# Mixture of experts: rows stored by slot and gathered back, in place of accumulating DMAs

## The chip, the cores and the metric

The kernel runs on one core of a Trainium2 chip. A core has five engines that work side by side and meet at semaphores: TensorE (PE) multiplies matrices, VectorE (DVE) and ScalarE (ACT) do elementwise work, GpSimd (POOL) does elementwise work and issues DMAs whose addresses come from a table in SBUF, and SyncE (SP) issues plain DMAs. The metric is the device time of one execution, in microseconds (us); the median of several runs counts.

## The reference

The network is a chain of six residual layers over 1024 tokens of 256 floats: mixture of experts, attention, mixture of experts, sparse feed-forward, a state-space layer, sparse feed-forward. The change touches the mixture of experts, which runs twice. The reference computes it like this, `x` being the normalised tokens:

```python
E, TOPK, H, I = (8, 2, 256, 512)
logits = SOFTCAP * jnp.tanh(x @ w_gate / SOFTCAP)
probs = jax.nn.softmax(logits, axis=-1)
_, idx = jax.lax.top_k(probs, TOPK)
mask = jax.nn.one_hot(idx, E, dtype=probs.dtype).sum(-2)
weights = probs * mask
for e in range(E):
    h = jax.nn.silu(x @ w1[e]) * (x @ w3[e])
    out = out + h @ w2[e] * weights[:, e:e + 1]
# and outside: x = x + 0.5 * layer(layernorm(x))
```

Each token so gets the sum of two experts' outputs, and only these two are needed.

## The kernel before

`moe_layer` runs only the experts that were picked. The 1024 tokens times 2 picks are sorted by expert into 23 items (`ITEMS`) of 128 slots each; each expert's last item is filled up with spare slots. A slot belongs to one (token, pick) pair. The layer has these stages:

1. VectorE makes the normalised tokens `xn` (L315). POOL stores them in DRAM as `rows` (L266). SP stores the residual in DRAM as `sums` (L253) and then loads the weights of all eight experts, 24 DMAs of 512 KB (L256, L258).
2. The router (L318 to L389) works out for every (token, pick) its slot (`slot`, L365), and from it three tables by slot: `token`, the token number or a spare row, `slot_w`, its weight, and `expert_of`, the expert of each item.
3. The item loop. POOL gathers an item's 128 token rows by an indirect DMA (`gather`, L272, four items ahead at most). TensorE turns them (L506), multiplies by the gate and up weights (L511), turns the product (L533) and multiplies by the down weights (L541). ScalarE and VectorE stand between these steps (L437, L443, L397, L449). VectorE weighs the 128 output rows into `y` (`weigh`, L406; two buffers), and POOL adds them into `sums` in DRAM by an accumulating indirect DMA (`add_rows`, L282). Two such adds may touch the same token, so each waits until the one before has landed (`summed`, L281).
4. When all 23 adds have landed, SP loads `sums` back into the residual (L261), and VectorE takes the statistics for the next layer's normalisation (`token_stats`, L75), eight tiles of 128 tokens.

TensorE starts its first multiplication only when all 24 weight loads have landed (`pe.wait_ge(q[loaded], 16 * EXPERTS)`). Each layer is a block of its own: no engine enters the next layer's block before all have left this one. On each engine instructions run in the order in which they are written. `routing_tables` prepares constants, and stores zeros in the spare rows of `rows` and `sums` (L2343).

Of the kernel before, what the change touches and what calls it, by code (L numbers as in the profile page):

```python
# [9 lines left out]
F32 = mybir.dt.float32  # L10
F32R = mybir.dt.float32r
BF16 = mybir.dt.bfloat16
U32 = mybir.dt.uint32
I32 = mybir.dt.int32
ALU = mybir.AluOpType
# [3 lines left out]
P = 128  # L19
D = 256  # L20
S = 1024
TT = S // P
# [143 lines left out]
CHOICES = 2  # L166
# [4 lines left out]
AHEAD = 4  # L171


def moe_layer(nc, xres, stats, ident, route, w_gate, w1, w3, w2, rows, sums, pool_dma, tag):

# [4 lines left out]
    with ExitStack() as ctx:  # L182
# [26 lines left out]
        place = sp.sb("place", [P, TT, EXPERTS])  # L209
        slot1 = sp.sb("slot1", [P, PICKS])  # L210
        slot = sp.sb("slot", [P, PICKS], I32)
        slot_item = sp.sb("slot_item", [P, PICKS], I32)
        slot_row = sp.sb("slot_row", [P, PICKS], I32)
        in_row = sp.sb("in_row", [P, PICKS, P], F32R)
# [18 lines left out]
        xT_ps = sp.ps("xT", [P, BANK])  # L233
        hT_ps = sp.ps("hT", [P, KI, P])
        out_ps = [sp.ps(f"out{b}", [P, BANK]) for b in range(2)]
        turn_banks = [gate_ps[0], gate_ps[1], up_ps[0], up_ps[1]]
        logit_ps, rank_ps, total_ps, slot_ps = out_ps[0], out_ps[1], xT_ps, hT_ps

        names = ("wg_loaded", "gate_loaded", "up_loaded", "down_loaded", "sums_stored",
                 "eps_done", "mv_done", "std_done", "rstd_done", "xn_done", "turned", "xnT_done", "logits_done",  # L240
                 "capped_done", "exp_done", "router", "both_done", "totals_done", "ranks_done",
                 "row_done", "send_done", "slots_done", "expert_done", "token_done", "slot_w_done",
                 "x_turned", "xT_done", "gate_done", "up_done", "silu_done", "h_done", "h_turned",
                 "hT_done", "out_done", "y_done", "reloaded")
        q = {n: sp.sem(n) for n in names}
        gathered, rows_stored, summed = pool_dma["gathered"], pool_dma["rows_stored"], pool_dma["summed"]
        ctx.callback(sp.clear_sems)
        block = ctx.enter_context(nc.Block())

        @block.sync  # L250
        def _(sync):
            sync.dma_start(wg[:], w_gate.rearrange("(k p) e -> p k e", p=P)).then_inc(q["wg_loaded"], 16)
            sync.dma_start(sums[0:S, :].rearrange("(t p) d -> p t d", p=P), xres).then_inc(q["sums_stored"], 16)  # L253
            for e in range(EXPERTS):
                for name, src, loaded in (("gate_up", w1, "gate_loaded"), ("up", w3, "up_loaded")):
                    sync.dma_start(w_in[name][:, e * KD:(e + 1) * KD, :], src[e].rearrange("(k p) n -> p k n", p=P)  # L256
                                   ).then_inc(q[loaded], 16)
                sync.dma_start(w_dn[:, e * KI:(e + 1) * KI, :], w2[e].rearrange("(k p) n -> p k n", p=P)  # L258
                               ).then_inc(q["down_loaded"], 16)
            sync.wait_ge(summed, 16 * ITEMS)  # L260
            sync.dma_start(xres, sums[0:S, :].rearrange("(t p) d -> p t d", p=P)).then_inc(q["reloaded"], 16)  # L261

        @block.gpsimd
        def _(pool):
            pool.wait_ge(q["xn_done"], TT)
            nc.gpsimd.dma_start(rows[0:S, :].rearrange("(t p) d -> p t d", p=P), xn[:]).then_inc(rows_stored, 16)  # L266

            def gather(i):
                b = i % AHEAD
                if i >= AHEAD:  # L270
                    pool.wait_ge(q["x_turned"], i - AHEAD + 1)
                nc.gpsimd.indirect_dma_start(out=xg[b][:], out_offset=None, in_=rows[:, :],  # L272
                                             in_offset=bass.IndirectOffsetOnAxis(ap=token[:, i:i + 1], axis=0)
                                             ).then_inc(gathered[b], 16)

            def add_rows(i):
                pool.wait_ge(q["y_done"], i + 1)
                if i == 0:
                    pool.wait_ge(q["sums_stored"], 16)
                else:  # L280
                    pool.wait_ge(summed, 16 * i)  # L281
                nc.gpsimd.indirect_dma_start(out=sums[:, :],  # L282
                                             out_offset=bass.IndirectOffsetOnAxis(ap=token[:, i:i + 1], axis=0),
                                             in_=y[i % 2][:], in_offset=None, compute_op=ALU.add
                                             ).then_inc(summed, 16)

            pool.wait_ge(rows_stored, 16)
            pool.wait_ge(q["token_done"], 1)
            for i in range(AHEAD):
                gather(i)  # L290
            for i in range(ITEMS):
                add_rows(i)
                if i + AHEAD < ITEMS:
                    gather(i + AHEAD)

        @block.vector
        def _(dve):
# [64 lines left out]
                                                ALU.mult, ALU.add))  # L362
            then(nc.vector.tensor_tensor(share[:], pick[:], place[:].unsqueeze(1).broadcast_to(cells), ALU.mult))
            then(nc.vector.tensor_reduce(slot1[:], share[:].rearrange("p k t e -> p (k t) e"), AX_X, ALU.add))
            then(nc.vector.tensor_scalar(slot[:], slot1[:], -1.0, None, ALU.add))  # L365
            nc.vector.tensor_scalar(slot_row[:], slot[:], P - 1, None, ALU.bitwise_and).then_inc(q["router"], 1)
            nc.vector.tensor_scalar(slot_item[:], slot[:], 7, None, ALU.logical_shift_right).then_inc(q["router"], 1)
# [31 lines left out]
            def weigh(i):  # L399
                b = i % 2  # L400
                dve.wait_ge(q["out_done"], i + 1)
                if i == 0:
                    dve.wait_ge(q["slot_w_done"], 1)
                if i >= 2:
                    dve.wait_ge(summed, 16 * (i - 1))
                nc.vector.tensor_scalar(y[b][:], out_ps[b][:, 0:D], slot_w[:, i:i + 1], None, ALU.mult).then_inc(q["y_done"], 1)  # L406

            for i in range(ITEMS):
# [1 line left out]
                if i:  # L410
                    weigh(i - 1)
            weigh(ITEMS - 1)
            dve.wait_ge(q["reloaded"], 16)
            token_stats(nc, stats, xres, range(TT))

        @block.scalar
        def _(act):
# [1896 lines left out]
def routing_tables(nc, keep, xres, ident, stats, x, ident_in, triangle, places):  # L2314
# [2 lines left out]
    route = dict(places=keep.sb("places", [P, P]), token1=keep.sb("token1", [P, PICKS]), spare1=keep.sb("spare1", [P, 1]),  # L2317
                 fills=keep.sb("fills", [P, EXPERTS]), ones=keep.sb("ones", [P, EXPERTS]),
                 ones_bf=keep.sb("ones_bf16", [P, P], BF16), upper=keep.sb("upper", [P, P], BF16))
    route["dram"] = [[nc.dram_tensor(f"moe{n}_{what}", (ROWS, D), F32).ap() for what in ("rows", "sums")] for n in range(2)]  # L2320
    with ExitStack() as ctx:
        sp = Space(nc, ctx, "main")
        eights = sp.sb("eights", [P, EXPERTS])
# [10 lines left out]
        @block.sync  # L2334
        def _(sync):
            sync.dma_start(xres[:], x.rearrange("b (t p) d -> p (b t) d", p=P)).then_inc(loaded, 16)
            sync.dma_start(ident[:], ident_in).then_inc(loaded, 16)
            sync.dma_start(eights[:], places.partition_broadcast(P)).then_inc(loaded, 16)
            sync.dma_start(upper_f[:], triangle).then_inc(upper_in, 16)
            sync.wait_ge(cleared, 1)  # L2340
            for n in range(2):
                for scratch in route["dram"][n]:
                    sync.dma_start(scratch[S:ROWS, :], zeros[:]).then_inc(spare_rows, 16)  # L2343
            sync.wait_ge(loaded, 48)
            sync.wait_ge(spare_rows, 64)

        @block.gpsimd
        def _(pool):
# [21 lines left out]
def macaron_kernel(nc, x, out, ident_in, triangle, mask, places, cos_t, sin_t, moe_gate, moe_w1, moe_w3, moe_w2,  # L2370
                   w_qkv, w_o, ffn_gate, ffn_up, ffn_down, in_w, conv_w, conv_b, dt_bias, a_log, d_skip, norm_w, out_w):
    with ExitStack() as ctx:
        sp = Space(nc, ctx, "main")
        xres = sp.sb("residual", [P, TT, D])
        ident = sp.sb("ident", [P, P])
        stats = sp.sb("token_stats", [P, TT, 6])
        stored = sp.sem("stored")
        pool_dma = [dict(gathered=[sp.sem(f"moe{n}_gathered{b}") for b in range(AHEAD)],
                         rows_stored=sp.sem(f"moe{n}_rows_stored"), summed=sp.sem(f"moe{n}_summed")) for n in range(2)]
        with ExitStack() as routing:  # L2380
            route = routing_tables(nc, Space(nc, routing, "route"), xres, ident, stats, x, ident_in, triangle, places)
            moe = (moe_gate, moe_w1, moe_w3, moe_w2)
            moe_layer(nc, xres[:], stats[:], ident[:], route, *moe, *route["dram"][0], pool_dma[0], "moe0")
            attention_layer(nc, xres[:], stats[:], ident[:], cos_t, sin_t, w_qkv, w_o, "attn")
            moe_layer(nc, xres[:], stats[:], ident[:], route, *moe, *route["dram"][1], pool_dma[1], "moe1")
        sparse_ffn_layer(nc, xres[:], stats[:], ident[:], ffn_gate, ffn_up, ffn_down, "ffn0")
        mamba_layer(nc, xres[:], stats[:], ident[:], triangle, mask, in_w, conv_w, conv_b, dt_bias, a_log, d_skip, norm_w,
                    out_w, "ssm")
        sparse_ffn_layer(nc, xres[:], stats[:], ident[:], ffn_gate, ffn_up, ffn_down, "ffn1", is_last=True)

        with nc.Block() as block:
            @block.sync
            def _(sync):
                sync.dma_start(out.rearrange("b (t p) d -> p (b t) d", p=P), xres[:]).then_inc(stored, 16)
                sync.wait_ge(stored, 16)
# [42 lines left out]
```

## Time and profile before

| what | us |
|---|---|
| median of 3 runs (lowest, highest) | 1891.13 (1887.7, 1897.0) |
| the profiled execution's own time | 1888.53 |
| its span (first to last instruction) | 1886.6 |
| PE busy | 1592.8 (84%) |
| DVE busy | 1151.1 (61%) |
| ACT busy | 862.5 (46%) |
| POOL busy | 440.5 (23%) |

All starts in the rows below are microseconds from the span's start, and durations are those of this one execution. The first mixture-of-experts layer lies at 10.5 to 208, the second at 721.5 to 920. "Idle before" in square brackets is how long the engine had stood idle and whose end released it. PEclk is the granted clock of TensorE: 1.00 is 2.4 GHz, 0.50 is 1.2 GHz.

### The profile page before, as it was taken

Reading aid. Unit: us, or ns where it says so; the run is one execution under the profiler, and the core shown is the slowest. Engines: PE = TensorE matmul, PEld = TensorE weight load, DVE = VectorE, ACT = ScalarE, POOL = GpSimd, SP = SyncE. Lnnn points to the kernel's source line nnn. Section 1 sums busy time; section 2 is a strip of 40 time slices with the busy share of each in tenths; the row PEclk is TensorE's granted clock in tenths of the full one; section 3 lists DMA queues with packets and bytes.
Section 4 is the critical chain, followed back from the end, with each engine's and each line's share of the span. In section 5 each row is a group of like instructions: output and inputs, shape, how many; then the busy total and the mean of one; then the engine's idle time right before and its main releaser. Section 6 shows DMA issues by size and latency. Waiting matters only on the chain. (4 is left out here: it accounts for less than half of the span.)

```text
span 1886.6 us, 25249 instructions
## 1 busy us (share of the span) xinstructions
PE 1592.8 (84%) x8136; PEld 1136.7 (60%) x8136; DVE 1151.1 (61%) x2072; ACT 862.5 (46%) x1270; POOL 440.5 (23%) x358
## 2 busy tenths in 40 slices
PE   3899389999999994799487786899999989988686
PEld 3466244454444444466376675787878878877575
DVE  3112578887878844121388574676776676675586
ACT  1122226665556571122232665666665666564232
POOL 1243320000000001244200111444444345343100
PEclk9999769999999996899798897999999999999798
DMA  8322110000000007322300100100100000010200
GB/s 306 76 47 44 43 23 8 5 12 12 11 12 11 0 1 241 102 47 43 98 1 0 40 17 13 29 18 23 29 18 23 26 13 28 12 29 12 67 1 23
DMA packets 70247, 73.78 MB, mean 39 GB/s; under 512 B 8384, under 2 KB 56896, under 8 KB 70144
## 3 DMA queue, kind: packets, MB, share of 16 engines
q1 hardware_dynamic: 60768, 58.35, 10.2%
q0 software_dynamic: 9376, 14.16, 4.3%
q8 instruction: 51, 0.84, 0.2%
q14 instruction: 52, 0.43, 0.1%
HBM read 56.50 MB, written 11.80 MB: 36 GB/s over the span
## 5 line engine op out<-in xcount | busy, mean ns | idle before, releaser
L779 DVE TENSOR_REDUCE attn_max_halves<-attn_scores 128x1 f32<-128x512 f32 x470 | 302.5, 686 | 69.8 <-PE attn_scores L1003 62.2
L908 ACT ACTIVATE attn_probs<-attn_scoresT 128x1024 f32<-128x1024 f32 x256 | 253.3, 1025 | 171.2 <-PE attn_scoresT L1016 170.8
L1003 PE MATMUL attn_scores<-attn_k_picks,attn_qT_pass 128*128 128x512 f32 x470 | 197.7, 452 | 5.7 <-DVE attn_max_halves L779 3.5
L1003 PEld LDWEIGHTS attn_scores<-attn_k_picks,attn_qT_pass 128*128 128x128 f32 x470 | 81.6, 188 | 152.4 <-DVE attn_max_halves L779 146.7
L1016 PE MATMUL attn_scoresT<-attn_qT_pass,attn_k_picks 128*128 128x512 f32 x512 | 168.7, 404 | 0.8 <-DVE attn_max_halves L779 0.8
L397 DVE TENSOR_TENSOR moe_h<-moe_silu,moe_up 128x512 f32<-128x512 f32 x46 | 31.6, 688 | 212.0 <-PE moe_up L511 212.0
L1442 DVE SCALAR_TENSOR_TENSOR ssm_scan_x<-ssm_scan_proj,ssm_w_conv,ssm_scan_x 128x1023 f32<-128x1023 f32 (+2 forms) x96 | 122.9, 1280 | 60.2 <-ACT ssm_scan_x L1437 57.1
L1030 PE MATMUL attn_o<-attn_probs,attn_v_group 128*32 128x512 f32 x1024 | 136.4, 605 | 0.6 <-ACT attn_probs L908 0.6
L443 ACT ACTIVATE moe_silu<-moe_gate 128x512 f32<-128x512 f32 x46 | 27.5, 598 | 223.1 <-PE moe_gate L511 223.1
L62 PE MATMUL ssm_scan_proj<-ssm_xnT_hi,ssm_w_in_hi 128*128 128x512 f32 x256 | 115.3, 450 | 5.6 <-POOL ssm_scan_mask L1920 5.4
L282 POOL DMA_INDIRECT moe_sums<-moe_y,moe_token x46 | 73.1, 1588 | 188.4 <-DVE moe_y L406 182.1
L2270 PE MATMUL ssm_scan_out<-ssm_scan_w_out,ssm_scan_v 128*128 128x256 f32 x464 | 114.1, 394 | 2.7 <-issue 2.7
L511 PE MATMUL moe_gate<-moe_w_gate_up,moe_xT 128*128 x184 | 90.3, 614 | 24.5 <-DMA moe_w_down<-in_moe_w 12.3
L2137 ACT ACTIVATE ssm_scan_decay<-ssm_scan_cum,ssm_neg_cum 128x128 f32<-128x128 f32 x256 | 73.3, 369 | 76.5 <-PE ssm_scan_cum L2207 76.5
L1016 PEld LDWEIGHTS attn_scoresT<-attn_qT_pass,attn_k_picks 128*128 128x128 f32 x512 | 93.9, 188 | 22.4 <-ACT attn_probs L908 4.4
L64 PE MATMUL ssm_scan_proj<-ssm_xnT_hi,ssm_w_in_lo 128*128 128x512 f32 x256 | 105.6, 412 | 0.0
L63 PE MATMUL ssm_scan_proj<-ssm_xnT_lo,ssm_w_in_hi 128*128 128x512 f32 x256 | 105.5, 412 | 0.0
L2270 PEld LDWEIGHTS ssm_scan_out<-ssm_scan_w_out,ssm_scan_v 128*128 128x128 f32 x464 | 91.5, 199 | 16.1 <-issue 2.8
L1924 POOL TENSOR_TENSOR ssm_w_in_lo<-ssm_w_in,ssm_w_in_hi 128x512 fp32r<-128x512 f32 x31 | 42.3, 1365 | 235.1 <-ACT ssm_w_in_hi L2101 235.1
L541 PE MATMUL moe_out<-moe_w_down,moe_hT 128*128 x368 | 87.1, 380 | 1.5 <-ACT moe_hT L449 1.5
L2026 DVE SCALAR_TENSOR_TENSOR ssm_scan_x<-ssm_scan_x,ssm_d_skip,ssm_scan_y 128x1024 f32<-128x1024 f32 x32 | 41.0, 1280 | 77.5 <-PE ssm_scan_y L2248 77.5
L541 PEld LDWEIGHTS moe_out<-moe_w_down,moe_hT 128*128 128x128 f32 x368 | 69.8, 190 | 30.2 <-issue 23.1
(338 smaller groups left out, 3414.5 us busy)
## 6 DMA issues: line engine op xcount, KB each, us to landing
moe_w_gate_up<-in_moe_w SPq DMA_DIRECT2D x16, 512.0 KB, 11.3
moe_w_up<-in_moe_w SPq DMA_DIRECT2D x16, 512.0 KB, 11.1
moe_w_down<-in_moe_w SPq DMA_DIRECT2D x16, 512.0 KB, 11.4
ssm_w_in<-in_in_w SPq DMA_DIRECT2D x64, 128.0 KB, 2.2
attn_k_picks<-attn_kT SPq DMA_DIRECT2D x32, 128.0 KB, 2.4
ssm_scan_w_out<-in_out_w SPq DMA_DIRECT2D x8, 512.0 KB, 4.1
moe_sums<-main_residual SPq DMA_DIRECT2D x2, 1024.0 KB, 5.7
moe_rows<-moe_xn POOLq DMA_DIRECT2D x2, 1024.0 KB, 9.9
```

The source lines that it names most:

```text
L62: nc.tensor.matmul(out, lhs_hi, rhs_hi, start=start, stop=False)
L63: nc.tensor.matmul(out, lhs_hi, rhs_lo, start=False, stop=False)
L64: return nc.tensor.matmul(out, lhs_lo, rhs_hi, start=False, stop=stop)
L511: last = nc.tensor.matmul(bank[:].unsqueeze(1), xT[i % 2][:, k, :], w_in[name][:, bass.ds(e * KD + k, 1), :], start=(k == 0), stop=(k == K ...
L541: last = nc.tensor.matmul(out_ps[i % 2][:, 0:D].unsqueeze(1), hT[i % 2][:, k, :], w_dn[:, bass.ds(e * KI + k, 1), :], start=(k == 0), stop ...
L779: return nc.vector.tensor_reduce(rmax2[:, t, j, c:c + 1], chunk_bank(g, n), AX_X, ALU.max).then_inc(reduced, 1)
L908: nc.scalar.activation(probs[s % 2][:, 2 * pair:2 * pair + 2, :], st_ps[pair][:], ACT.Exp, scale=SCALE).then_inc(exp_done, 1)
L1003: nc.tensor.matmul(chunk_bank(g, n), qm[b][:, t * P:(t + 1) * P], kz[b][:, j, c * BANK:(c + 1) * BANK], start=True, stop=True).then_inc(sc ...
L1016: last = nc.tensor.matmul(st_ps[pair][:, j % 2, :], kz[b][:, j, kt * P:(kt + 1) * P], qe[b][:, half * BANK:(half + 1) * BANK], start=True, ...
L1030: last = nc.tensor.matmul(o_ps[j * STACK:(j + 1) * STACK, :], vg[b][:, kt, :], probs[s % 2][:, j, :], start=(kt == 0), stop=(kt == KT_TILE ...
L1442: return nc.vector.scalar_tensor_tensor(out[:, shift:], ps[:, :S - shift], w(k), out[:, shift:], ALU.mult, ALU.add)
L2270: last = nc.tensor.matmul(out[:, m, :], v[:, v_row(b * NORM_HEADS + jn), cols], w_out[:, jn, :], start=(jn == 0), stop=(jn == NORM_HEADS - 1))
```

## The change

The residual no longer goes to DRAM. `sums` is replaced by a DRAM tensor `slots` with one row for each of the 23 x 128 slots. SP stores each weighted item `y` there by a plain DMA (23 of 128 KB), with a semaphore for each of the two buffers. POOL first issues all gathers of token rows; when all items are stored, it gathers, for each of the eight token tiles, the two slots of each token (`take_back`, 16 indirect DMAs of 128 rows) into SBUF that the layer no longer needs (`xn` and `xnT`). VectorE then adds the two rows to the residual, tile by tile, and takes each tile's statistics. The router writes `slot1 - 1` once more, as an unsigned integer, for these gathers.

```diff
-            sync.dma_start(sums[0:S, :].rearrange("(t p) d -> p t d", p=P), xres).then_inc(q["sums_stored"], 16)
...
-            sync.wait_ge(summed, 16 * ITEMS)
-            sync.dma_start(xres, sums[0:S, :].rearrange("(t p) d -> p t d", p=P)).then_inc(q["reloaded"], 16)
+            for i in range(ITEMS):
+                sync.wait_ge(q["y_done"], i + 1)
+                sync.dma_start(slots[i * P:(i + 1) * P, :], y[i % 2][:]).then_inc(y_stored[i % 2], 16)
+            for b in range(2):
+                sync.wait_ge(y_stored[b], 16 * ((ITEMS + 1 - b) // 2))
...
-            def add_rows(i):
-                pool.wait_ge(q["y_done"], i + 1)
-                if i == 0:
-                    pool.wait_ge(q["sums_stored"], 16)
-                else:
-                    pool.wait_ge(summed, 16 * i)
-                nc.gpsimd.indirect_dma_start(out=sums[:, :],
-                                             out_offset=bass.IndirectOffsetOnAxis(ap=token[:, i:i + 1], axis=0),
-                                             in_=y[i % 2][:], in_offset=None, compute_op=ALU.add
-                                             ).then_inc(summed, 16)
+            def take_back(t, k):
+
+                at = k * TT + t
+                nc.gpsimd.indirect_dma_start(out=picked[k][:, t, :], out_offset=None, in_=slots[:, :],
+                                             in_offset=bass.IndirectOffsetOnAxis(ap=slot_u[:, at:at + 1], axis=0)
+                                             ).then_inc(combined[t], 16)
...
-            for i in range(ITEMS):
-                add_rows(i)
-                if i + AHEAD < ITEMS:
-                    gather(i + AHEAD)
+            for i in range(AHEAD, ITEMS):
+                gather(i)
+            for b in range(2):
+                pool.wait_ge(y_stored[b], 16 * ((ITEMS + 1 - b) // 2))
+            for t in range(TT):
+                for k in range(CHOICES):
+                    take_back(t, k)
...
+            nc.vector.tensor_scalar(slot_u[:], slot1[:], -1.0, None, ALU.add)
             then(nc.vector.tensor_scalar(slot[:], slot1[:], -1.0, None, ALU.add))
...
                 if i >= 2:
-                    dve.wait_ge(summed, 16 * (i - 1))
+                    dve.wait_ge(y_stored[b], 16 * (i // 2))
...
-            dve.wait_ge(q["reloaded"], 16)
-            token_stats(nc, stats, xres, range(TT))
+            for t in range(TT):
+                dve.wait_ge(combined[t], 32)
+                for k in range(CHOICES):
+                    then(nc.vector.tensor_tensor(xres[:, t, :], picked[k][:, t, :], xres[:, t, :], ALU.add))
+                token_stats(nc, stats, xres, (t,))
...
-                for scratch in route["dram"][n]:
-                    sync.dma_start(scratch[S:ROWS, :], zeros[:]).then_inc(spare_rows, 16)
+                sync.dma_start(route["dram"][n][0][S:ROWS, :], zeros[:]).then_inc(spare_rows, 16)
```

SP at the start of the first layer, before: the store of the residual stands ahead of the weights.

```order
L252 DMA moe0_w_gate<-in_moe_gate 128x2x8
L253 DMA moe0_sums<-main_residual 128x8x256
L256 DMA moe0_w_gate_up<-in_moe_w1 128x2x512
L256 DMA moe0_w_up<-in_moe_w3 128x2x512
L258 DMA moe0_w_down<-in_moe_w2 128x4x256
```

The same place after.

```order
L255 DMA moe0_w_gate<-in_moe_gate 128x2x8
L258 DMA moe0_w_gate_up<-in_moe_w1 128x2x512
L258 DMA moe0_w_up<-in_moe_w3 128x2x512
L260 DMA moe0_w_down<-in_moe_w2 128x4x256
```

One DMA of 1024 KB is gone from the head of the queue; the 24 weight loads follow in the same order.

POOL at the end of the first layer, before: the last gather of token rows (`x_rows`) and the accumulating DMAs.

```order
L272 DMA moe0_x_rows2<-moe0_rows,moe0_token 128x256 [waits moe0_x_turned]
L282 DMA moe0_sums<-moe0_y1,moe0_token 1152x256 [waits main_moe0_summed,moe0_y_done]
L282 DMA moe0_sums<-moe0_y0,moe0_token 1152x256 [waits main_moe0_summed,moe0_y_done]
L182 UNCONDITIONAL_BRANCH
L49 UNCONDITIONAL_BRANCH [waits barrier_Pool_Activation_PE_DVE_SP_gather]
```

The same place after, the first two of the 16 gathers back (into `xn` and `xnT`).

```order
L277 DMA moe0_x_rows2<-moe0_rows,moe0_token 128x256 [waits moe0_x_turned]
L284 DMA moe0_xn<-moe0_slots,moe0_slot_u 128x256 [waits moe0_y_stored1,moe0_y_stored0]
L284 DMA moe0_xnT<-moe0_slots,moe0_slot_u 128x256
L182 UNCONDITIONAL_BRANCH
L49 UNCONDITIONAL_BRANCH [waits barrier_Pool_Activation_PE_DVE_SP_gather]
```

Of the 16 gathers the first pair stands here; the pair is issued eight times, and only its first instruction waits. All of them stand behind the last item's store.

VectorE at the end of the first layer, before.

```order
L406 TENSOR_SCALAR moe0_y0<-moe0_out0,moe0_slot_w 128x256 [waits main_moe0_summed,moe0_out_done]
L75 BN_STATS main_token_stats<-main_residual 128x6 [waits moe0_reloaded]
L75 BN_STATS main_token_stats<-main_residual 128x6 x7
L182 UNCONDITIONAL_BRANCH
L758 UNCONDITIONAL_BRANCH [waits barrier_Pool_Activation_PE_DVE_SP_release]
```

The same place after, with the last of the eight tiles.

```order
L411 TENSOR_SCALAR moe0_y0<-moe0_out0,moe0_slot_w 128x256 [waits moe0_y_stored0,moe0_out_done]
...
L421 TENSOR_TENSOR main_residual<-moe0_xn,main_residual 128x256 [waits main_moe0_combined7]
L421 TENSOR_TENSOR main_residual<-moe0_xnT,main_residual 128x256 [waits moe0_router]
L75 BN_STATS main_token_stats<-main_residual 128x6 [waits moe0_router]
L182 UNCONDITIONAL_BRANCH
L766 UNCONDITIONAL_BRANCH [waits barrier_Pool_Activation_PE_DVE_SP_release]
```

The eight statistics waited for one load; now each tile has its own wait, two additions and its statistics.

## Rows read from the trace of the kernel before

**Rows 1.** The page's part 1: busy time and share of each engine.
```profile
PE 1592.8 (84%) x8136; PEld 1136.7 (60%) x8136; DVE 1151.1 (61%) x2072; ACT 862.5 (46%) x1270; POOL 440.5 (23%) x358
```

**Rows 2.** Item loop: stretch, PE, PEld, DVE, ACT, POOL busy, PEclk, DMA share, GB/s.
```profile
100.00:150.00 50.00, 50.00 (x189) 31.47 (x188) 10.54 (x18) 10.98 (x25) 21.34 (x17) 1.00 0.30 48
```

**Rows 3.** Timeline of one item of the loop: start, duration, engine, line.
```profile
73.64 1.88 PE L511 MATMUL moe_gate<-moe_w_gate_up,moe_xT 128*128 x4
73.85 0.48 DVE L406 TENSOR_SCALAR moe_y<-moe_out,moe_slot_w 128x256 f32<-128x256 f32 x1 [0.99 <-PE moe_out L541]
...
74.61 1.60 POOL L282 DMA_INDIRECT moe_sums<-moe_y,moe_token  x1 [2.89 <-DVE moe_y L406]
...
76.51 0.98 POOL L272 DMA_INDIRECT moe_x_rows<-moe_rows,moe_token  x1 [0.30 <-PE moe_xT L506]
...
79.46 1.02 PE L511 MATMUL moe_gate<-moe_w_gate_up,moe_xT 128*128 x2
```

**Rows 4.** Timeline, start of both layers: residual store, first gate multiplication.
```profile
10.96 0.46 SPq L253 DMA_DIRECT2D moe_sums<-main_residual  x1
...
56.45 1.21 PE L511 MATMUL moe_gate<-moe_w_gate_up,moe_xT 128*128 x1 [12.23 <-issue]
...
767.48 3.78 PE L511 MATMUL moe_gate<-moe_w_gate_up,moe_xT 128*128 x4 [12.30 <-DMA moe_w_down<-in_moe_w]
```

**Rows 5.** Busy time by stretch, while the weights load; the last column is GB/s.
```profile
12.00:16.00 4.00, 2.62 (x13) 2.62 (x14) 3.03 (x10) 1.69 (x5) 0.21 (x1) 1.00 0.97 262
20.00:55.00 35.00, 8.95 (x52) 8.16 (x51) 11.85 (x61) 2.14 (x4) 3.90 (x4) 1.00 1.03 363
723.00:727.00 4.00, 2.61 (x12) 2.61 (x13) 3.03 (x10) 1.70 (x5) 0.21 (x1) 0.50 1.01 283
```

**Rows 6.** Timeline, end of the first layer.
```profile
193.17 0.48 DVE L406 TENSOR_SCALAR moe_y<-moe_out,moe_slot_w 128x256 f32<-128x256 f32 x1 [2.71 <-PE moe_out L541]
...
195.33 1.55 POOL L282 DMA_INDIRECT moe_sums<-moe_y,moe_token  x1 [3.04 <-DMA moe_sums<-moe_y,moe_token]
199.01 0.37 SPq L261 DMA_DIRECT2D main_residual<-moe_sums  x1
204.59 2.71 DVE L75 BATCH_NORM_STATS2 main_token_stats<-main_residual 128x6 f32<-128x256 f32 x8 [10.93 <-DMA main_residual<-moe_sums]
```

**Rows 7.** Timeline, end of the second layer.
```profile
916.91 2.71 DVE L75 BATCH_NORM_STATS2 main_token_stats<-main_residual 128x6 f32<-128x256 f32 x8 [11.06 <-DMA main_residual<-moe_sums]
```

**Rows 8.** Timeline, first layer: the token table, and three of the first four gathers.
```profile
36.48 0.18 DVE L387 SCALAR_TENSOR_TENSOR moe_token<-moe_hT,moe_empty 128x24 uint32<-128x24 f32 x1
...
37.55 1.05 POOL L272 DMA_INDIRECT moe_x_rows<-moe_rows,moe_token  x1 [20.63 <-DVE moe_token L387]
...
38.91 0.95 POOL L272 DMA_INDIRECT moe_x_rows<-moe_rows,moe_token  x1 [0.30 <-issue]
...
41.42 0.95 POOL L272 DMA_INDIRECT moe_x_rows<-moe_rows,moe_token  x1 [0.30 <-issue]
```

**Rows 9.** DMA issues: size of each, median us from issue to landing.
```profile
ssm_w_in<-in_in_w SPq DMA_DIRECT2D x64, 128.0 KB, 2.2
...
out<-main_residual SPq DMA_DIRECT2D x1, 1024.0 KB, 4.4
...
moe_x_rows<-moe_rows,moe_token POOLq DMA_INDIRECT x46, 2.8
...
moe_rows<-main_zeros SPq DMA_DIRECT2D x2, 128.0 KB, 4.0
```

**Rows 10.** Instructions on VectorE by shape: busy total, mean ns of one.
```profile
L1226 DVE TENSOR_TENSOR ffn_xT_lo<-ffn_xT,ffn_xT_hi 128x256 fp32r<-128x256 f32 x16 | 6.7, 418 | 0.1
```

**Rows 11.** One line's instructions: ns min/median/max, first and last start.
```profile
L118 DVE TENSOR_SCALAR attn_xn<-main_residual,attn_ln_mean_var,attn_ln_rstd x8: 395/407/5366, 214.1 to 221.5; 128x256 f32<-128x256 f32 x8
```

**Rows 12.** Busy time by stretch where TensorE restarts after the layer; PEclk third from the end.
```profile
222.00:224.00 2.00, 2.00 (x10) 2.00 (x10) 1.81 (x3) 1.47 (x3) 0.00 (x0) 0.51 0.00 0
224.00:226.00 2.00, 1.85 (x11) 1.52 (x9) 1.45 (x4) 0.44 (x3) 0.00 (x0) 1.00 0.00 0
```

More of the change, by code:

```diff
@@ L171, with moe_layer @@
 AHEAD = 4
-def moe_layer(nc, xres, stats, ident, route, w_gate, w1, w3, w2, rows, sums, pool_dma, tag):
+def moe_layer(nc, xres, stats, ident, route, w_gate, w1, w3, w2, rows, slots, pool_dma, tag):
     with ExitStack() as ctx:
@@ L211, in moe_layer @@
         slot = sp.sb("slot", [P, PICKS], I32)
+        slot_u = sp.sb("slot_u", [P, PICKS], U32)
         slot_item = sp.sb("slot_item", [P, PICKS], I32)
@@ L235, in moe_layer @@
         out_ps = [sp.ps(f"out{b}", [P, BANK]) for b in range(2)]
+        picked = [xn, xnT[:].rearrange("p k (a d) -> p (k a) d", d=D)]
         turn_banks = [gate_ps[0], gate_ps[1], up_ps[0], up_ps[1]]
         logit_ps, rank_ps, total_ps, slot_ps = out_ps[0], out_ps[1], xT_ps, hT_ps
-        names = ("wg_loaded", "gate_loaded", "up_loaded", "down_loaded", "sums_stored",
+        names = ("wg_loaded", "gate_loaded", "up_loaded", "down_loaded",
                  "eps_done", "mv_done", "std_done", "rstd_done", "xn_done", "turned", "xnT_done", "logits_done",
@@ L243, in moe_layer @@
                  "x_turned", "xT_done", "gate_done", "up_done", "silu_done", "h_done", "h_turned",
-                 "hT_done", "out_done", "y_done", "reloaded")
+                 "hT_done", "out_done", "y_done")
         q = {n: sp.sem(n) for n in names}
-        gathered, rows_stored, summed = pool_dma["gathered"], pool_dma["rows_stored"], pool_dma["summed"]
+        y_stored = [sp.sem(f"y_stored{b}") for b in range(2)]
+        gathered, rows_stored, combined = pool_dma["gathered"], pool_dma["rows_stored"], pool_dma["combined"]
         ctx.callback(sp.clear_sems)
@@ L2319, in routing_tables @@
                  ones_bf=keep.sb("ones_bf16", [P, P], BF16), upper=keep.sb("upper", [P, P], BF16))
-    route["dram"] = [[nc.dram_tensor(f"moe{n}_{what}", (ROWS, D), F32).ap() for what in ("rows", "sums")] for n in range(2)]
+    route["dram"] = [[nc.dram_tensor(f"moe{n}_{what}", (size, D), F32).ap() for what, size in (("rows", ROWS), ("slots", ITEMS * P))]
+                     for n in range(2)]
     with ExitStack() as ctx:
@@ L2341, in _ @@
             for n in range(2):
-                for scratch in route["dram"][n]:
-                    sync.dma_start(scratch[S:ROWS, :], zeros[:]).then_inc(spare_rows, 16)
+                sync.dma_start(route["dram"][n][0][S:ROWS, :], zeros[:]).then_inc(spare_rows, 16)
             sync.wait_ge(loaded, 48)
-            sync.wait_ge(spare_rows, 64)
+            sync.wait_ge(spare_rows, 32)
         @block.gpsimd
@@ L2378, in macaron_kernel @@
         pool_dma = [dict(gathered=[sp.sem(f"moe{n}_gathered{b}") for b in range(AHEAD)],
-                         rows_stored=sp.sem(f"moe{n}_rows_stored"), summed=sp.sem(f"moe{n}_summed")) for n in range(2)]
+                         rows_stored=sp.sem(f"moe{n}_rows_stored"), combined=[sp.sem(f"moe{n}_combined{t}") for t in range(TT)]) for n in range(2)]
         with ExitStack() as routing:
```

## The prediction, made before the changed kernel ran

> **What bounds the kernel now.** I read the page's busy times first: TensorE is busy 84% of the span [rows 1]. That average says little here, because each layer is closed off from the next; so I looked at the three stages of a mixture-of-experts layer.
>
> The item loop comes first. The stretches show TensorE busy 50.00 of 50 us, with POOL at 21.34 and DMA at 0.30 [rows 2]. From one item's gate multiplication (73.64) to the next (79.46) go 5.82 us, and in them POOL's add and gather end at 77.49, so it then stands idle until the next `y` [rows 3]. TensorE alone sets the pace; the 23 adds are hidden, except the last.
>
> The start is next. TensorE's first multiplication starts at 56.45 after 12.23 us of idleness, in the second layer at 767.48, released by the last weight load [rows 4]. Until then the DMA engines are full, at 363 GB/s [rows 5]. What the DMA engines carry ahead of the last weight moves this start.
>
> Last the end. The last `y` is ready at 193.65 (193.17 + 0.48). Its add is issued at 195.33, because the add before it must have landed; it lands before 199.01, where SP issues the load; the statistics start at 204.59 and end at 207.30 [rows 6]. So 13.65 us pass with TensorE idle; in the second layer VectorE stands idle for 11.06 us before its statistics, the first 10.93 [rows 6, 7]. No engine does other work there: every microsecond of this chain is on the path.
>
> **The change, part by part.**
>
> *Start: the store of the residual goes.* Its 1024 KB head the queue (issued at 10.96, [rows 4]). From 12 to 16 the DMA engines move 262 GB/s x 4 us = 1.05 MB, just this store's size; in the second layer 1.13 MB in the 4 us from 723 [rows 5]. So the store holds the queue for about 4 us, and the weights follow it. The least that it can be worth is its bytes at the later rate, 1.05 MB / 363 GB/s = 2.9 us; the most is those 4.0 us plus some of its issue, 4.3. I take 3.6 for each layer, nearer to the measured stretch, with a little off since weight reads may already run under its last writes. Two layers: -7.2 us. The start stays bound by the weights: the first four gathers are issued by 42.4 [rows 8], long before.
>
> *The additional `slot_u` and the two missing stores of zeros: 0.* `slot_u` delays the token table by 0.1 to 0.2 us, at 36.66 [rows 8]; the weights, for which TensorE waits until 56.45, hide it, 3.6 us of gain included. If they didn't, it would cost 0.2 us a layer. The zeros are queued behind the loads for which the first statistics wait; gone, they are worth at least 0 and at most the 0.5 us of an issue.
>
> *Loop: adds out of POOL, stores into SP: 0.* POOL has idle time already. `weigh` of item i now waits for the store of item i-2, 11.6 us earlier (2 x 5.82), which takes 2 to 4 us. Behind a late one would queue VectorE's next product, and TensorE behind that; the cover is about 7 us. SP has nothing else to issue by then. I exclude a gain because TensorE has no idle time to give back [rows 2].
>
> *End: add, wait and reload go; store, 16 gathers and additions come.* The new chain in the first layer, with before's times for what comes ahead:
>
> - The store of the last `y` (128 KB, plain, SP). The trace has no such store alone. From below: the 1024 KB store of the output lands in 4.4, less the 0.92 MB more that it moves, 2.5 us at 363 GB/s, is 1.9. From above: the 128 KB stores of zeros at the start, queued behind others, take 4.0. A 128 KB load takes 2.2 [rows 9]. I take 2.3: landed at 195.95.
> - POOL sees it. From a `y` ready at 74.33 to its add at 74.61 pass 0.28 us [rows 3]; from the token table (36.66) to the first gather 0.89 [rows 8]. I take 0.6: first gather at 196.55.
> - Sixteen gathers. They are the same operation as those of token rows (128 rows of 1 KB). Queued one behind the other these start 1.255 us apart (38.91 to 41.42, two steps), 0.95 busy and 0.30 between; both steps are POOL's own, since nothing is waited for [rows 8]. The last starts 15 x 1.255 = 18.8 us after the first, at 215.4. From below, the 0.30 could vanish: 0.95 each. From above, each could take as long as an accumulating one, 1.60 [rows 3] and 0.30: 1.9.
> - The last lands 2.8 after its issue [rows 9], at 218.2.
> - The last tile's two additions and statistics. The nearest addition, 128x256, takes 0.418 [rows 10], with a semaphore between I take 0.45; the statistics 2.71 / 8 = 0.34, say 0.4 alone. Together 1.3: 219.5. The other seven tiles' work (1.3 every 2.5 us) lies under the gathers.
>
> 219.5 against 207.30 is +12.2 us for a layer, +24.4 for both. Everything after it (the barrier, the next layer) follows with the same distances.
>
> The clock: TensorE restarts after the layer at 1.2 GHz (0.51 of 222 to 224) and is at 2.4 GHz from 224 [rows 12]. It had fallen in the idle time already, so 12 us more of idleness add nothing I can price; one such ramp, four microseconds at half the clock, is the size of error that I allow.
>
> **Sum.** 24.4 - 7.2 = +17.2 us on the profiled execution's 1888.5 gives 1905.7. Its span is 1886.6, and the 1.9 around it stays. That execution lies 2.6 us under the median of the three runs, 1891.1; from the median the sum would be 1908.3. I predict 1907, between.
>
> **A rule of the skill against the row.** The row shows a gather every 1.255 us [rows 8]. The Trainium skill, page "DMA: Bandwidth & Descriptors", section "Anatomy of one DMA — SWDGE (gpsimd) path", says that descriptor generation is small and that the cost of a DMA is a fixed 2 us, mostly the wait for the write's receipt, plus bytes over 436 GB/s. By that rule the 16 gathers would overlap and take only what their bytes take, an estimate of 16 x 0.3 us. The trace doesn't agree for gathers by index; the case stands among the rivals.
>
> **The rivals.**
>
> *Data-bound gathers (faster).* If 16 queued gathers were paced by their data and not by POOL, at 128 KB (0.131 MB) / 363 GB/s = 0.36 us each, the last would be issued 5.4 us after the first in place of 18.8: each layer 13.4 us shorter, and the sum 17.2 - 26.8 = -9.6, 1879 on the profiled base. It speaks for it that the DMA engines are idle then; against it that POOL is busy 0.95 us for each gather even where nothing holds it, 0.95 and 1.05 at the start, 0.98 in the loop [rows 3, 8]. The page named above would give this case.
>
> *Gathers at their busy time (no change that can be told).* With 0.95 each and no gap, 15 x 0.305 x 2 = 9.2 less: +8.0, about 1897 to 1899. For it: the gap is called "issue", nothing known. Against: it stands in both steps, and 0.30 also in the loop. The change only pays below 0.68 us a gather, where the 15 steps save the 8.6 us (12.2 - 3.6) by which each layer else grows.
>
> *Gathers and additions hinder each other (slower still).* In the new tail, and nowhere before, gathers run beside VectorE additions with both inputs in SBUF. One `attn_xn` took 5.366 us against a median of 0.407 [rows 11], so some instructions of VectorE and POOL do shut each other out. If each gather lost one addition's time (0.42), 15 x 0.42 x 2 = 12.6 more: 1920. The Trainium skill, page "SBUF — State Buffer", section "Who interferes with whom", says that such a tensor_tensor contends with GpSimd's reads, while descriptor generation needs the write side; by that nothing is lost.
>
> *Only a few gathers may be in flight.* Four in a row is all that the trace shows. Were each to wait for the one before to land, 2.8 in place of 1.255: 15 x 1.55 x 2 = 46 more, 1953.
>
> *The weights don't come earlier.* If the start stayed where it is, 7.2 more: 1914. It is part of the forecast's range.
>
> **How the numbers follow.** The forecast has 0.75; its own terms leave 1898 to 1915 (start 2.9 to 4.3, store 1.9 to 4.0, pick-up 0.3 to 0.9, each twice; the gathers' step a tenth either way is 3.8; the base 2.6). Hindered gathers 0.07, few in flight 0.03; gathers without the gap 0.10; data-bound 0.05. The range reaches down to the case without the gap and up to the hindered one: 1896 to 1919. A measurement of this kernel can tell a change from about 0.5%, 9.5 us, on: below 1881.7 is faster, over 1900.6 slower. Faster 0.05; within 0.11 (the gapless case and the forecast's lower edge); slower 0.84.
>
> **What would show it.** The first gate multiplication would start 3.6 us earlier (about 52.9), items still every 5.8 us; from the last `y` to the end of the last statistics 25.9 us in place of 13.65; 16 gathers 1.25 us apart, each waiting for nothing; SP's stores of `y` landing in about 2.3; VectorE idle before each tile's first addition, released by a gather. The forecast is wrong if the gathers' step is under 0.8 or over 1.6, or if the item loop slows down.

## The result, and the profile after

The changed kernel takes 1913.68 us (median; 1912.06 to 1915.51), the kernel before beside it 1889.7. The ratio is 1.0099, with a 95% interval of 1.0072 to 1.0127; the two medians alone give 1.0127, the edge of it. Timed again later, six runs beside 17 of before, it is 1.0114 (1.0086 to 1.0143). So the change costs about 1%, some 20 us. Of 17 executions of the kernel before that were timed with the first four variants below, four were slow ones of 2712 to 5370 us; no ratio counts them. The profiled execution took 1913.1 us, with a span of 1911.3.

First the start of both layers after the change, from the timeline; it answers to [rows 4].

```profile
11.04 0.46 SPq L258 DMA_DIRECT2D moe_w_gate_up<-in_moe_w  x1
...
53.55 3.77 PE L519 MATMUL moe_gate<-moe_w_gate_up,moe_xT 128*128 x4 [12.04 <-issue]
...
779.22 1.21 PE L519 MATMUL moe_gate<-moe_w_gate_up,moe_xT 128*128 x1 [13.21 <-DMA moe_w_down<-in_moe_w]
```

The weights' first DMA is now at the head of the queue, and the first gate multiplication starts at 53.55, where it was 56.45. The second layer as a whole lies later now, so it is measured from its own start below.

The item loop by stretch: stretch, PE, PEld, DVE, ACT and POOL busy, PEclk, DMA share, GB/s.

```profile
100.00:150.00 50.00, 50.00 (x192) 31.32 (x191) 9.86 (x17) 11.72 (x26) 7.64 (x9) 1.00 0.14 45
```

TensorE is as full as in [rows 2]. POOL has 7.64 us of work in place of 21.34, and DMA 0.14 in place of 0.30, but the loop is no shorter.

The end of the first layer, timeline of POOL and VectorE; it answers to [rows 6].

```profile
191.07 0.48 DVE L411 TENSOR_SCALAR moe_y<-moe_out,moe_slot_w 128x256 f32<-128x256 f32 x1 [2.71 <-PE moe_out L549]
193.53 0.95 POOL L284 DMA_INDIRECT moe_xn<-moe_slots,moe_slot_u  x1 [36.78 <-DMA moe_slots<-moe_y]
194.78 0.95 POOL L284 DMA_INDIRECT moe_xnT<-moe_slots,moe_slot_u  x1 [0.30 <-issue]
196.04 0.95 POOL L284 DMA_INDIRECT moe_xn<-moe_slots,moe_slot_u  x1 [0.30 <-issue]
197.30 0.95 POOL L284 DMA_INDIRECT moe_xnT<-moe_slots,moe_slot_u  x1 [0.30 <-issue]
197.56 0.42 DVE L421 TENSOR_TENSOR main_residual<-moe_xn,main_residual 128x256 f32<-128x256 f32 x1 [6.00 <-DMA moe_xnT<-moe_slots,moe_slot_u]
198.01 0.42 DVE L421 TENSOR_TENSOR main_residual<-moe_xnT,main_residual 128x256 f32<-128x256 f32 x1
198.47 0.43 DVE L75 BATCH_NORM_STATS2 main_token_stats<-main_residual 128x6 f32<-128x256 f32 x1
198.55 0.96 POOL L284 DMA_INDIRECT moe_xn<-moe_slots,moe_slot_u  x1 [0.30 <-issue]
...
212.44 0.96 POOL L284 DMA_INDIRECT moe_xnT<-moe_slots,moe_slot_u  x1 [0.30 <-issue]
...
215.26 0.42 DVE L421 TENSOR_TENSOR main_residual<-moe_xn,main_residual 128x256 f32<-128x256 f32 x1 [1.27 <-DMA moe_xnT<-moe_slots,moe_slot_u]
215.72 0.42 DVE L421 TENSOR_TENSOR main_residual<-moe_xnT,main_residual 128x256 f32<-128x256 f32 x1
216.18 0.43 DVE L75 BATCH_NORM_STATS2 main_token_stats<-main_residual 128x6 f32<-128x256 f32 x1
218.05 0.21 POOL L728 MEMSET attn_k_stack<- 128x128 f32 x1 [4.66 <-POOLq L48]
```

The 16 gathers stand in one row, 1.26 us apart, and wait for nothing; VectorE finishes a tile and idles until the next pair lands. From the last `y` (191.55) to the end of the statistics (216.61) pass 25.06 us, where it was 13.65. TensorE idles through all of it.

DMA issues of the changed kernel: size, median us from issue to landing.

```profile
moe_slots<-moe_y SPq DMA_DIRECT2D x46, 128.0 KB, 1.7
```

Now the whole span in stages, each from its first VectorE instruction to that of the next. The four untouched layers are taken together.

| stage, us | before | after | difference |
|---|---|---|---|
| first mixture-of-experts layer | 197.53 | 207.44 | +9.91 |
| second | 198.84 | 206.87 | +8.03 |
| both | 396.37 | 414.31 | +17.94 |
| attention, feed-forward twice, state space | 1479.66 | 1486.31 | +6.65 |

Within the two layers: block start to first gate multiplication -3.0 and -2.1; item loop +0.8 and -1.4; last `y` to end of statistics +11.4 and +11.2; from there to the next block +0.7 and +0.3. So the layers that were changed give 17.9 us. The 6.7 us more (6.8 in the expectations below, from starts read to 0.1 us) lie in layers whose code is the same, and had to be explained.

### The profile page after: what moved, and what is told of

It reads as the page before. It is cut to its first block and busy times, and to the rows that moved or that the text cites. A ratio compares the mean times of both kernels' runs of the same rounds, so it can differ in the third digit from the quotient of the medians.

```text
span 1911.3 us, 25269 instructions
## 1 busy us (share of the span) xinstructions
PE 1591.0 (83%) x8136; PEld 1133.5 (59%) x8136; DVE 1164.6 (61%) x2106; ACT 862.7 (45%) x1270; POOL 397.7 (21%) x344
## 5 line engine op out<-in xcount | busy, mean ns | idle before, releaser
L277 POOL DMA_INDIRECT moe_x_rows<-moe_rows,moe_token x46 | 44.0, 956 | 235.6 <-PE moe_xT L514 198.1
## 6 DMA issues: line engine op xcount, KB each, us to landing
moe_w_up<-in_moe_w SPq DMA_DIRECT2D x16, 512.0 KB, 11.2
moe_w_down<-in_moe_w SPq DMA_DIRECT2D x16, 512.0 KB, 11.2
```

## The experiments

Three variants of the changed kernel ask what paces the gathers. In each, the times meant are those from the last `y` to the end of the statistics.

**One pick only.** 8 gathers a layer.

```diff
-                for k in range(CHOICES):
-                    take_back(t, k)
+                take_back(t, 0)
...
-                dve.wait_ge(combined[t], 32)
-                for k in range(CHOICES):
+                dve.wait_ge(combined[t], 16)
+                for k in range(1):
```

> The changed kernel with only the first pick gathered back and added: 8 gathers a layer in place of 16; the second pick's rows are left out of the result. Theory (POOL paces the gathers, 1.26 us each): from the last y to the end of the last statistics 25.1 - 8 x 1.26 - 0.45 = 14.5 us in each layer, the whole some 21 us shorter than the changed kernel's 1913, 1892. Rival (the tail is mostly store, wake-up and landing, with the gathers overlapping): the tail shrinks by 4 us or less in each layer.

Measured: 14.54 and 14.44 us, and 1893.1 as a whole (one run). 25.0 - 14.5 = 10.5 us for 8 gathers and one addition of 0.45: 1.26 each. The theory's numbers held: each gather less makes the tail one step shorter.

**Half the bytes.** The table of slots then counts half rows.

```diff
-                nc.gpsimd.indirect_dma_start(out=picked[k][:, t, :], out_offset=None, in_=slots[:, :],
+                nc.gpsimd.indirect_dma_start(out=picked[k][:, t, 0:P], out_offset=None, in_=slots.rearrange("r (h d) -> (r h) d", h=2),
...
-            nc.vector.tensor_scalar(slot_u[:], slot1[:], -1.0, None, ALU.add)
+            nc.vector.tensor_scalar(slot_u[:], slot1[:], 2.0, -2.0, ALU.mult, ALU.add)
```

> The changed kernel, with each of the 16 gathers moving only the first 512 bytes of each row (128 rows as before; the other half of each row is left out of the result). Theory (POOL's work per instruction or per row sets the pace): the step stays 1.26 us and the tail 25 us. Rival (data-bound gathers): the step falls towards 0.65 us, the tail to some 16 us.

The gathers of this variant on POOL: ns min/median/max.

```profile
L284 POOL DMA_INDIRECT moe_xn<-moe_slots,moe_slot_u x16: 953/955/957, 192.3 to 935.7; - x16
L284 POOL DMA_INDIRECT moe_xnT<-moe_slots,moe_slot_u x16: 952/955/1186, 193.5 to 937.0; - x16
```

Measured: 0.955 busy with the same 0.30 between (one gather in each layer took 1.2, cause not known), and 24.97 and 25.03 us from the last `y` to the end. The whole is 1912.3 (one run). Half the data saves nothing. Data-bound gathers are refuted.

**Half the rows.**

```diff
-                nc.gpsimd.indirect_dma_start(out=picked[k][:, t, :], out_offset=None, in_=slots[:, :],
-                                             in_offset=bass.IndirectOffsetOnAxis(ap=slot_u[:, at:at + 1], axis=0)
+                nc.gpsimd.indirect_dma_start(out=picked[k][0:64, t, :], out_offset=None, in_=slots[:, :],
+                                             in_offset=bass.IndirectOffsetOnAxis(ap=slot_u[0:64, at:at + 1], axis=0)
```

> The changed kernel with gathers of 64 rows of 1 KB in place of 128 (the other 64 tokens of each tile are left out of the result). If POOL pays by the row, 0.95 busy becomes about 0.5 and the step 0.8 us, the tail 25.1 - 15 x 0.47 = 18 us. If it pays by the instruction, the step stays 1.26. Data-bound gathers would give the first result too, so it counts only beside the run with half the bytes.

The same rows of this variant:

```profile
L284 POOL DMA_INDIRECT moe_xn<-moe_slots,moe_slot_u x16: 904/908/912, 193.9 to 935.9; - x16
L284 POOL DMA_INDIRECT moe_xnT<-moe_slots,moe_slot_u x16: 910/914/918, 195.1 to 937.1; - x16
```

Measured: 0.91 busy for 64 rows against 0.957 for 128, and the tail 24.08 and 24.03; the whole is 1918.6 (one run; its untouched layers took 1493.1, which the last part of this section is about). By these two points 64 rows cost 0.05 us and the instruction itself about 0.86, with 0.30 before the next. POOL pays by the instruction. Each gather here takes one index per partition, 128 rows, so 2048 rows are 16 instructions; a gather of more rows is in no run.

Two experiments take the start apart.

**Late store, in the kernel before.** Only this line moves behind the weights' loop.

```diff
-            sync.dma_start(sums[0:S, :].rearrange("(t p) d -> p t d", p=P), xres).then_inc(q["sums_stored"], 16)
             for e in range(EXPERTS):
...
+            sync.dma_start(sums[0:S, :].rearrange("(t p) d -> p t d", p=P), xres).then_inc(q["sums_stored"], 16)
             sync.wait_ge(summed, 16 * ITEMS)
```

> The kernel before, with the residual's 1024 KB store issued after the 24 weight loads in place of ahead of them; nothing else changes. Theory (the start pays the store's bytes at the queue's rate): the first gate multiplication starts 2.9 us earlier in each layer, the store lands before the first add at 65, and the whole is 5.8 us (0.3%) shorter than before. Rival (the earlier start came from elsewhere in the change, the queue refills the gap): no more than 1 us. Rival 2 (the first add must now wait for the store): the item loop starts late and the gain is lost.

The first gate multiplication of both layers, timeline:

```profile
53.64 2.92 PE L511 MATMUL moe_gate<-moe_w_gate_up,moe_xT 128*128 x3 [9.43 <-issue]
...
762.68 3.78 PE L511 MATMUL moe_gate<-moe_w_gate_up,moe_xT 128*128 x4 [8.79 <-DMA moe_w_down<-in_moe_w]
```

Measured: block start to first gate multiplication 43.10 and 42.35 us, where before has 45.84 and 45.86: 2.7 and 3.5 earlier. The item loop isn't held up by the store (136.92 and 137.38 long, before 137.21 and 138.38). The ratio to before is 0.9981 (0.9960 to 1.0002); 0.9969 was expected and lies inside, but so does no change, just. The stage shows the gain; the whole is too noisy to.

**The store put back, in the changed kernel.**

```diff
+            sync.dma_start(rows_spare[0:S, :].rearrange("(t p) d -> p t d", p=P), xres).then_inc(q["sums_stored"], 16)
             for e in range(EXPERTS):
...
+            sync.wait_ge(q["sums_stored"], 16)
             for b in range(2):
```

> The changed kernel with the residual's 1024 KB store put back ahead of the weights (into a DRAM tensor nobody reads). Theory: the first gate multiplication starts 2.9 us later in the first layer and 2 to 3 later in the second, the whole 5 to 6 us over the changed kernel (about 1919). Rival (the weights' start doesn't depend on the store): same as the changed kernel.

Measured: first multiplication after 46.25 and 45.97 us, where the changed kernel has 42.87 and 43.77: 3.4 and 2.2 later. The tail stays (25.05, 24.98), and the two changed layers take 419.7 us, 5.3 over the changed kernel. The median of four runs is 1917.3, 1.0120 of before (1.0095 to 1.0144). Beside the changed kernel it wasn't timed, and that interval overlaps the changed kernel's: again the stage shows the store, and the whole doesn't. Its untouched layers took 1478.4 us.

That last number was the first sign on the 6.7 us: a variant of the changed kernel whose untouched layers are as short as before's.

**Idle time added to the kernel before**, to move the later layers to where the changed kernel has them.

```diff
-            sync.wait_ge(summed, 16 * ITEMS)
+            sync.wait_ge(q["padded"], 1)
...
+            pool.wait_ge(summed, 16 * ITEMS)
+            cells = {"moe0": 11550, "moe1": 9330}[tag]
+            for at in range(0, cells, 4096):
+                idle = w_in["up" if at < 8192 else "gate_up"][:].rearrange("p a n -> p (a n)")
+                last = nc.gpsimd.memset(idle[:, at % 8192:at % 8192 + min(4096, cells - at)], 0.0)
+            last.then_inc(q["padded"], 1)
```

> The kernel before, with idle time added to the end of both layers: after the last add has landed POOL clears 11550 columns (9.9 us) in the first and 9330 (8.0 us) in the second before SP may reload. That brings the next layers to nearly the same places in time as in the changed kernel. The layers nobody touched (attention, both feed-forward layers, state space) took 6.8 us more in the changed kernel's profile than before. Theory (the granted clock falls at other moments when these layers start later): they take some us more than before here too, 3 to 8, and the whole is 21 to 26 us over before. Rival (the change itself slows them, by its code, its DMAs or where its data lies): they take before's time within 1 us and the whole is 18 us over. Rival 2 (chance from run to run): either, and the runs of one kernel spread by as much.

The second variant has 5800 and 4650 columns in the place of 11550 and 9330.

> As the run with idle time, with half as much (5.0 and 4.0 us). Theory (clock): the untouched layers again differ from before's by several us, not necessarily half as much and of either sign. Rival (the change itself): 0 within 1 us, the whole 9 us over before.

Measured: with 10 us of idleness the two padded layers take 208.2 and 207.4, the untouched ones 1489.6, the whole 1.0102 of before (1.0077 to 1.0127), 19.5 us by the medians. With half of it 203.0, 201.9 and 1489.6, the whole 1.0056 (1.0034 to 1.0078). The whole doesn't decide: 19.5 us lies between the 18 of the rival and the 21 to 26 of the theory, and the interval reaches both, also for the half (10.5 us by the medians, where the rival said 9). The profiles say more. The untouched layers are 10 us over the first profile of before, in a kernel with none of the change's DMAs, and just as much with half the delay. So such a growth needs no part of the change. But "as much for either delay" also speaks against a fixed effect of where the layers start, and for chance. The same two programs, profiled again, test that.

> The kernel before, profiled once more. Its four untouched layers took 1479.6 us in the first profile, and 1484.1 to 1489.6 in the four variants of it. Theory (chance: the moments at which the granted clock falls and rises differ from run to run): some 1485, with 5 either way, not 1479.6 again; the changed layers 197.5 and 198.9 within 1.5. Rival (each program has its own fixed pattern): 1479.6 within 1 us.

> The changed kernel, profiled once more and timed beside the kernel before. Theory (chance): untouched layers some 1485 us with 5 either way, as in the kernel before; over many runs the changed kernel is longer by the changed layers' 17.9 us alone, a ratio of 1.0095. Rival (the change slows the untouched layers): 1486 or more again, and 24 us longer, a ratio of 1.013.

Measured, in the second profiles: the kernel before 198.0 and 197.5, untouched layers 1486.0 (first profile 1479.7). The changed kernel 206.3 and 206.5, untouched layers 1486.5 (first profile 1486.3). The same program thus differs by 6.4 us where nothing was changed, and the second profiles differ by 0.5 there and by 17.3 in the changed layers. The rival of a fixed pattern fell. The 17 executions of before in that series go from 1884.8 to 1898.95, and the ratio of the same program to itself came out as 1.0011 (0.9996 to 1.0025).

The rival that the change slows the untouched layers is not refuted by the whole time: 1.0114 (1.0086 to 1.0143) lies between its 1.013 and the theory's 1.0095, and holds both. The profiles speak against it. The untouched layers took 1479.7 to 1489.7 us in the six of the kernel before and its variants, 1485.6 on average, and 1478.4 to 1493.1 in the six of the changed kernel and its variants, 1486.2 on average. With such a spread an effect of some 5 us can't be excluded, but none is needed.

Where a part of this comes from can be seen in one place, the end of the attention layer, from 506 us after the layer's start on, in both profiles of the kernel before, as busy time by stretch. First profile:

```profile
714.14:721.60 7.46, 3.12 (x24) 2.94 (x24) 4.57 (x11) 0.00 (x0) 0.00 (x0) 1.00 0.00 0
```

Second profile:

```profile
715.00:726.00 11.00, 6.07 (x29) 5.49 (x27) 5.39 (x14) 1.17 (x2) 0.00 (x0) 0.66 0.00 0
```

The columns are as above; PEclk is third from the end. In the first profile TensorE keeps 2.4 GHz to the layer's end; in the second the granted clock is at 1.2 GHz in part of this stretch (0.66 on average). The whole layer takes 516.9 us in place of 513.5. At the stretch's start the second profile is already 1.1 us behind, at the same instruction; 2.3 are lost in the dip. The changed kernel's first profile has the same dip:

```profile
724.12:735.40 11.28, 6.16 (x30) 5.53 (x28) 5.29 (x12) 1.15 (x2) 0.00 (x0) 0.67 0.00 0
```

It is the same short stretch with gaps in TensorE's work; whether the clock falls in it differs between executions of one program. Here too 2.3 us are lost, beside 1.5 before. Of all twelve profiles nine lose 1.5 to 2.3 us in this place: all six of the changed kernel and its variants, and three of the six of before and its variants. It is one place out of several; that the rest of the 6.4 us is of the same kind is likely, but not shown.

**A version that beats both.** The experiments point to keeping the accumulating DMAs, with the late store as above, and a reload in eight DMAs with statistics tile by tile.

```diff
...
-            sync.dma_start(xres, sums[0:S, :].rearrange("(t p) d -> p t d", p=P)).then_inc(q["reloaded"], 16)
+            for t in range(TT):
+                sync.dma_start(xres[:, t, :], sums[t * P:(t + 1) * P, :]).then_inc(reloaded[t], 16)
...
-            dve.wait_ge(q["reloaded"], 16)
-            token_stats(nc, stats, xres, range(TT))
+            for t in range(TT):
+                dve.wait_ge(reloaded[t], 16)
+                token_stats(nc, stats, xres, (t,))
```

> The kernel before with the late store, and the reload cut into eight DMAs of one token tile each, with the statistics of a tile taken as soon as it has landed. Theory: of 2.71 us of statistics only the last 0.4 stay behind the last landing, while eight issues of 0.4 us cost the first landing little: 2 us less for each layer beside the 2.9 of the late store, the whole 9 to 10 us (0.5%) under before. Rival (eight small DMAs land later than one large, by their issue of 8 x 0.42 = 3.4 us): the tail stays within 1 us of before's, and only the late store's gain is left.

The end of its first layer, timeline:

```profile
192.18 1.55 POOL L284 DMA_INDIRECT moe_sums<-moe_y,moe_token  x1 [2.86 <-DMA moe_sums<-moe_y,moe_token]
195.82 3.66 SPq L263 DMA_DIRECT2D main_residual<-moe_sums  x8
197.99 1.25 DVE L75 BATCH_NORM_STATS2 main_token_stats<-main_residual 128x6 f32<-128x256 f32 x3 [7.30 <-DMA main_residual<-moe_sums]
199.52 0.76 DVE L75 BATCH_NORM_STATS2 main_token_stats<-main_residual 128x6 f32<-128x256 f32 x2 [0.28 <-DMA main_residual<-moe_sums]
200.96 1.15 DVE L75 BATCH_NORM_STATS2 main_token_stats<-main_residual 128x6 f32<-128x256 f32 x3 [0.68 <-DMA main_residual<-moe_sums]
```

Eight issues take 3.66 us, but the first tile's statistics start 2.17 after the first issue, where the one large load took 5.58. From the last `y` to the end of the statistics pass 11.43 and 11.86 us, where before has 13.65 and 13.77, a gain of 2.2 and 1.9. This stretch differs between executions too: beside the second profile of before (13.13 and 13.48) and the late store's (13.26 and 13.37) the gain is 1.5 to 1.8. The whole is 1885.1, and 0.9953 of before (0.9935 to 0.9971), as expected: 9 us faster than before. By the two ratios it is some 28 us faster than the changed kernel, beside which it wasn't timed.

## Why the prediction was right, point by point

The direction and the mechanism were right, the range (1896 to 1919) holds 1913.7, and the sum for the changed layers (+17.2) met the measured +17.9 and, in the second pair, +17.3. That it met them so closely is in part luck, since errors of up to 2.1 us cancel. For both layers together, measured against forecast: the start gave back 2.1 us less, the loop took 0.6 less, the end 1.8 less, and 1.0 came that had no term; 17.2 + 2.1 - 0.6 - 1.8 + 1.0 = 17.9. The span "1898 to 1915" of the forecast's own terms doesn't come out of them either: with every term at its bound they give 1899 to 1917.5. The terms in turn:

- *The start, -3.6 a layer.* Mis-sized: -3.0 and -2.1, in the late-store variant -2.7 and -3.5. Over the seven profiles without the store at the head, against the first of before, it is 1.7 to 3.5, 2.7 on average. The lower bound, the store's bytes at the later rate (2.9, [rows 5]), was the better price. The four microseconds in which only the store's bytes moved were not all lost to the weights.
- *The loop, 0.* +0.8 and -1.4. Over all profiles of all variants the loop took 136.8 to 138.5 us, so both lie within chance. The cover was real: stores of `y` land in 1.7 us.
- *The store of the last `y`, 2.3, and POOL's pick-up, 0.6.* Together 1.98 (191.55 to 193.53), 0.9 less than the 2.9 taken. The store landed 1.7 after its issue, under the lower bound of 1.9, and 0.3 is left for the rest.
- *The gathers.* 15 steps took 18.91 us (193.53 to 212.44); 18.8 was predicted from two steps of [rows 8]. The largest term was the best known. What follows the last issue took 4.17; 2.8 + 1.3 = 4.1 was said.
- *What wasn't priced.* The next block starts 0.7 and 0.3 us later behind the last statistics, in both pairs of profiles. With eight gathers it starts 1.26 us behind them in both layers, in place of 0.84 and 0.83; with POOL's clearing as its last work, in the variant with 10 us of idle time, 0.86. So it goes with the gathers, not with the idle time. The trace's barrier instructions show it on POOL: POOL joins the barrier 0.36 us after the last statistics in place of 0.06, in both layers, and in the first it clears the semaphores (L54) 0.45 after that barrier in place of 0.08. Why is open; POOL's last indirect DMA also ends only 3 us before the barrier here, and 10 us before it in the kernel before.
- *The base.* 1907 missed by 6.7 us, and 0.7 of them are the sum's. The rest is the base. The profiled execution, 1888.5, is no typical one: later series of the same kernel, on two chips, have medians of 1892.6 and 1896.8. From those the sum of 17.2 us gives 1910 to 1914. The spread of the three runs shown (9.3 us) said as much, and I averaged two low numbers in place of reading it.

The rivals: data-bound gathers and gathers at their busy time are refuted, since the gap of 0.30 stayed in all 30 steps and half the bytes changed nothing. The rule of the Trainium skill, page "DMA: Bandwidth & Descriptors", section "Anatomy of one DMA — SWDGE (gpsimd) path", holds in one part: that many descriptors cost little more (64 rows 0.05 us). It doesn't hold in what I drew from it, that the gathers then take only what their bytes take: each instruction occupies POOL for 0.96 of every 1.26 us. Gathers and additions don't hinder each other: a gather takes 0.95 before VectorE starts and 0.96 beside it, an addition 0.42. The Trainium skill, page "SBUF — State Buffer", section "Who interferes with whom", says that descriptor generation needs the write side that such an addition leaves free, and calls it inferred; the trace agrees. The rival of few in flight fell for this kernel: sixteen gathers in a row keep their step. As each lands 2.8 us after its issue, no more than three are in flight at once at 1.26 us, so what happens with more isn't shown. That the weights don't come earlier is refuted by the start, in both layers.

## What to carry to other kernels

Count the indirect DMAs that stand on the path, not their rows or bytes: here one costs 1.26 us of POOL whether it moves 64 KB or 128, and 1.21 with half the rows. Adds hidden under a full TensorE are worth nothing, however many they are; what follows the last item is worth everything, so move work out of the tail, not into it. And where untouched stages of the same program differ by several us between executions, take the base from several runs, and read a change from its own stage's time.

## What the runs showed of the hardware that was not expected

An indirect gather on POOL takes 0.957 us for 128 rows of 1 KB, 0.955 for 128 rows of 512 B, 0.91 for 64 rows of 1 KB, each with 0.30 us before the next. A plain 128 KB store to DRAM from SP lands in 1.7 us, faster than a 128 KB load of [rows 9] (2.2). The granted clock in the same stretch of the same program was 1.00 in one execution and 0.66 in another, which cost 2.3 us there. And a layer's end takes 1.1 to 1.6 us when gathers on POOL end some 3 us before the last statistics do, 0.8 to 0.9 in the kernel before and its variants.
